# Batches 0 and 1 kept split in DRAM, the second MLP seven steps behind, the last heads' scaling between two steps

## The reference

```python
# layer 0: cross attention (16 heads of 16), then an MLP
q = ln(x) @ Wq;  k, v = split(ln(context) @ Wkv)
x = x + softmax(q k^T * 0.25) v @ Wproj + bproj
x = x + gelu(ln(x) @ W1 + b1) @ W2 + b2
# layer 1: self attention (16 heads of 64), cross attention (16 of 64), gated MLP
x = attn(ln(x), ln(x), Wq1, Wk1, Wv1, Wo1, bo1) + x
x = attn(ln(x), context, Wq2, Wk2, Wv2, Wo2, bo2) + x
a, gate = split(ln(x) @ Wp + bp)
x = x + (a * gelu(gate)) @ Wf + bf
```

## Time and profile before

| | us |
|---|---|
| median of 3 runs | 2421.74 (2419.34 to 2422.18) |
| profiled execution | 2421.08 |
| its span | 2419.2 |
| PE busy | 2161.0 (89%) |
| DVE busy | 1674.4 (69%) |
| ACT busy | 1310.7 (54%) |
| POOL busy | 1292.6 (53%) |

### The profile page before, as it was taken

One profiled execution on the slowest core, in us unless ns is written; L12 is line 12 of the kernel. 1 busy time (PEld: TensorE's weight loads), 2 busy tenths in 40 slices (PEclk: granted clock), 3 DMA queues, 4 the chain that ended last, 5 costly groups with the idle time before them and its releaser, 6 DMA issues. The chain is left out here.

```text
span 2419.2 us, 31242 instructions
## 1 busy us (share of the span) xinstructions
PE 2161.0 (89%) x11628; PEld 1788.5 (74%) x11628; DVE 1674.4 (69%) x2343; ACT 1310.7 (54%) x1938; POOL 1292.6 (53%) x1013
## 2 busy tenths in 40 slices
PE   6867999997699999999999999999999689999998
PEld 4646888886577777777777777777777578899887
DVE  5457677654777777777777878777776776666654
ACT  5335666643466656565666665565665355555431
POOL 2145455545255556565555656656556676666432
PEclk8968999998899999999999999999999899999999
DMA  6610000011000000000000000000011321111000
GB/s 199 211 39 7 20 20 21 10 53 51 13 23 14 26 25 14 32 14 23 23 14 32 14 18 32 14 23 23 14 34 53 115 81 49 51 52 44 27 9 18
DMA packets 87608, 94.27 MB, mean 39 GB/s; under 512 B 29409, under 2 KB 69089, under 8 KB 87457
## 3 DMA queue, kind: packets, MB, share of 16 engines
q1 hardware_dynamic: 87456, 92.27, 11.7%
HBM read 61.30 MB, written 29.62 MB: 38 GB/s over the span
## 5 line engine op out<-in xcount | busy, mean ns | idle before, releaser
L144 PE MATMUL PS<-R 128*128 128x512 f32 (+1 forms) x2944 | 1033.4, 351 | 138.8 <-DVE R L160 52.5
L145 PE MATMUL PS<-R 128*128 128x512 f32 (+1 forms) x2944 | 1002.5, 341 | 0.0
L146 PE MATMUL PS<-R 128*128 128x512 f32 (+1 forms) x2944 | 1002.5, 341 | 0.0
L144 PEld LDWEIGHTS PS<-R 128*128 128x128 f32 x2944 | 570.5, 194 | 257.2 <-DVE R L160 68.6
L157 POOL TENSOR_SCALAR R<-F 128x1024 fp32r<-128x1024 f32 (+1 forms) x487 | 546.6, 1127 | 346.2 <-DVE F L1775 147.3
L154 ACT ACTIVATE R<-PS 64x512 fp32r<-64x512 f32 (+4 forms) x860 | 460.5, 546 | 385.4 <-PE PS L146 155.1
L146 PEld LDWEIGHTS PS<-R 128*128 128x128 f32 x2944 | 570.0, 194 | 61.6
L145 PEld LDWEIGHTS PS<-R 128*128 128x128 f32 x2944 | 571.7, 194 | 55.2
L160 DVE TENSOR_TENSOR R<-F,R 128x1024 fp32r<-128x1024 f32 (+2 forms) x426 | 528.6, 1245 | 79.0 <-POOL R L157 56.3
L1359 ACT ACTIVATE F<-PS 128x1024 f32<-128x1024 f32 x256 | 263.2, 1028 | 331.5 <-PE PS L1225 204.8
L160 DVE TENSOR_TENSOR R<-PS,R 128x512 fp32r<-128x512 f32 (+3 forms) x348 | 181.9, 543 | 232.4 <-ACT R L154 231.7
(11 more groups left out here) (85 smaller groups left out, 1900.1 us busy)
## 6 DMA issues: line engine op xcount, KB each, us to landing
F<-sd SPq DMA_DIRECT2D x128, 128.0 KB, 2.8
gd<-F SPq DMA_DIRECT2D x8, 1024.0 KB, 4.1
vd<-F SPq DMA_DIRECT2D x8, 1024.0 KB, 4.5
xs<-F SPq DMA_DIRECT2D x16, 512.0 KB, 2.6
F<-xs SPq DMA_DIRECT2D x16, 512.0 KB, 3.6
R<-gd SPq DMA_DIRECT2D x8, 1024.0 KB, 5.8
R<-vd SPq DMA_DIRECT2D x8, 1024.0 KB, 5.7
F<-in_x SPq DMA_DIRECT2D x8, 512.0 KB, 5.5
```

The costliest lines, as they stand in the source:

```text
L144: nc.tensor.matmul(o, L[0], Rr[0], start=start, stop=False, skip_group_check=share)
L145: nc.tensor.matmul(o, L[0], Rr[1], start=False, stop=False, skip_group_check=share)
L146: return nc.tensor.matmul(o, L[1], Rr[0], start=False, stop=stop, skip_group_check=share)
```

## The change

1. *Products.* Batches 0 and 1 get DRAM tensors of their own, `gd2` and `vd2`, that hold hi and lo. ACT rounds these two batches' part straight from PSUM to hi, DVE subtracts for lo, and SP writes both. The plain copies cover the other six batches. The groups of vw are taken in the order of batches 2-3, 4-5, 6-7, 0-1 (`vw5_pair`). The new buffers take the place of the stage in which the weights of this part arrived, so ACT first waits for these weights to be split.
2. *Stage 4, start.* Batches 0 and 1 are loaded as pairs, with twice the bytes, and PE waits for the load itself. Their splits (8 halves on ACT and POOL) are gone from `products_at` and from the outer loop.
3. *Lag.* LAG is 7: the loop has one step fewer, and batch b's first MLP block stands in step 4b+7. The norms stay where they are. The down-projection's residual additions and the stores follow the lag; the weights of the MLP are split one step earlier (4, 3, 3, 3, 3 a step).
4. *Last heads.* `early4_pool = {6: 1, 8: 2, 9: 1}`: on POOL alone, step 3 is moved behind the scaling of the last head pair.

The diff, cut to its core:

```diff
@@ -375,11 +377,14 @@
-            with nc.sbuf_tensor("R0", [128, 6528], FR) as r, nc.sbuf_tensor("F0", [128, 12288], FP) as g:
-                ra, fa = Area(r, 6528), Area(g, 12288)
+            with nc.sbuf_tensor("R0", [128, 6528], FR) as r, nc.sbuf_tensor("F0", [128, 6144], FP) as g:
+                ra, fa = Area(r, 6528), Area(g, 6144)
                 kt5, vb5 = [ra.pair(NT) for _ in range(2)], [ra.pair(8, 128) for _ in range(2)]
-                gs5, vs5 = [fa.take(8, 256) for _ in range(2)], [fa.take(8, 256) for _ in range(2)]
-                stage5 = fa.take(8 * 512)
+                gs5, vs5 = [fa.take(6, 256) for _ in range(2)], [fa.take(6, 256) for _ in range(2)]
+                with nc.sbuf_tensor("S0", [128, 4096], FP) as stage5_at:
+                    stage5 = Area(stage5_at, 4096).take(4096)
+                with nc.sbuf_tensor("S1", [128, 4096], FR) as split5:
+                    gr5, vr5 = [[shaped(split5, 2048 * k + 1024 * i, (2, 2, 256)) for i in range(2)] for k in range(2)]
...
@@ -473,10 +480,13 @@ (sp_products)
-                nc.sync.dma_start(gd[:, :, p, :].rearrange("b p w -> p b w"), gs5[p % 2]).then_inc(g5_out[p % 2].sem, 16)
+                nc.sync.dma_start(gd[2:, :, p, :].rearrange("b p w -> p b w"), gs5[p % 2]).then_inc(g5_out[p % 2].sem, 16)
+                sp.wait_ge(g5_lo, 2 * p + 1)
+                nc.sync.dma_start(gd2[:, :, p].rearrange("b p h w -> p b h w"), f32(gr5[p % 2])).then_inc(g5_out[p % 2].sem, 16)
...
@@ -567,13 +582,19 @@ (act_products)
                 if p >= 0:
+                    wait_weights(act, "k2", "q2", "v2", "o2")
                     act.wait_ge(g5_out[p % 2], p // 2 - 1)
                     act.wait_ge(g5_mm, 2 * p)
                     act_copy(g5_view(gs5[p % 2], 0), g5_bank(0)).then_inc(g5_act.sem, 1)
+                    act_copy(g5_view(gr5[p % 2][:, :, 0, :], 0), g5_bank(0, 0, 2)).then_inc(g5_hi.sem, 1)
+                    act.wait_ge(g5_mm, 2 * p + 1)
+                    act_copy(g5_view(gr5[p % 2][:, :, 0, :], 1), g5_bank(1, 0, 2)).then_inc(g5_hi.sem, 1)
...
+                    act.wait_ge(vw5_mm, 4 * p + 3)
+                    act_copy(vr5[p % 2][:, :, 0, :], vw5_bank(3)).then_inc(vw5_hi.sem, 1)
@@ -608,12 +629,17 @@ (dve_products)
-                    dve.wait_ge(g5_mm, 2 * p + 1)
-                    nc.vector.tensor_copy(g5_view(gs5[p % 2], 1), g5_bank(1)).then_inc(g5_dve.sem, 1)
+                    for k in range(2):
+                        dve.wait_ge(g5_hi, 2 * p + k)
+                        if k == 1:
+                            nc.vector.tensor_copy(g5_view(gs5[p % 2], 1), g5_bank(1)).then_inc(g5_dve.sem, 1)
+                        hi, lo = [g5_view(gr5[p % 2][:, :, h, :], k) for h in range(2)]
+                        dve_rest(lo, g5_bank(k, 0, 2), hi).then_inc(g5_lo.sem, 1)
...
@@ -1115,15 +1141,35 @@
         def sp_keys(b):
...
+            if b < 2:
+                nc.sync.dma_start(to, gd2[b]).then_inc(g_in[b].sem, 16)
+            else:
+                nc.sync.dma_start(to[:, :, 1, :], gd[b]).then_inc(g_in[b % 2].sem, 16)
...
+        def wait_keys(queue, b):
+
+            if b < 2:
+                queue.wait_ge(g_in[b], 0)
+            else:
+                queue.wait_ge(g_lo, 2 * b - 3)
...
-        early4 = {6: 1, 8: 3}
+        early4, early4_pool = {6: 1, 8: 3}, {6: 1, 8: 2, 9: 1}
...
@@ -1395,9 +1441,6 @@ (act_attention1)
-                    if tail3(s, j) == 4:
-                        act_keys(0, 0)
-                        act_keys(0, 1)
...
@@ -1530,10 +1573,7 @@ (pool_attention1)
-                    if tail3(s, j) == 4:
-                        pool_keys(0, 0)
-                        pool_keys(0, 1)
-                    for _ in range(early4.get(tail3(s, j), 0)):
+                    for _ in range(early4_pool.get(tail3(s, j), 0)):
                         next(ahead)
...
-        N4, LAG = 4 * NB, 8
+        N4, LAG = 4 * NB, 7
...
         def products_at(i):
 
-            if i == 1:
-                return [("k", 1, 0), ("v", 0, 0), ("v", 0, 1)]
-            if i in (3, 4, 5):
-                return [[], [("v", 1, 0)], [("v", 1, 1), ("k", 2, 0)]][i - 3]
             kind, b = ("k", i // 4 + 1) if i % 4 in (1, 2) else ("v", (i + 1) // 4)
-            return [(kind, b, int(i % 4 in (0, 2)))] if 1 < i and b < NB else []
+            return [(kind, b, int(i % 4 in (0, 2)))] if 2 <= b < NB else []
 
         def weights_at(i):
-            return g5[3 * i - 6:3 * i - 3] if 2 <= i < LAG else []
+            return g5[3 * i - 5 if i > 2 else 0:3 * i - 2] if 2 <= i < LAG else []
...
-                if i % 4 == 0 and i >= LAG + 4:
+                if (i - LAG) % 4 == 0 and i >= LAG + 4:
                     sp_store(3, (i - LAG - 4) // 4, out, res4, 2 * ((i - LAG - 4) // 4) + 1)
...
-                pe.wait_ge(g_lo, 2 * b + 1)
+                wait_keys(pe, b)
```

More of the change, by code:

```diff
@@ L452, in build @@
         g5_mm, g5_act, g5_dve = event("g_mm", 16), event("g_act", 8), event("g_dve", 8)
+        g5_hi, g5_lo, vw5_hi = event("g_hi", 16), event("g_lo", 16), event("vw_hi", 8)
         vw5_mm, vw5_act, vw5_dve = event("vw_mm", 32), event("vw_act", 16), event("vw_dve", 16)
-        g5_out = [event(f"g_out{i}", 4, 16) for i in range(2)]
-        vw5_out = [event(f"vw_out{i}", 4, 16) for i in range(2)]
+        g5_out = [event(f"g_out{i}", 4, 32) for i in range(2)]
+        vw5_out = [event(f"vw_out{i}", 4, 32) for i in range(2)]
         def sp_products():
@@ L523, in pe_products @@
                         pe.wait_ge(yn_hi, 1)
-                        for b in (2 * i, 2 * i + 1):
+                        for b in (2 * vw5_pair(i), 2 * vw5_pair(i) + 1):
                             m = mm3(bank(6 + i % 2)[:, 256 * (b % 2):256 * (b % 2) + 256], [v[:, b, :] for v in vb5[p % 2]],
@@ L530, in g5_view, with g5_bank, vw5_pair @@
             return v.rearrange("p b (k a s) -> p k a b s", k=2, a=2)[:, k]
-        def g5_bank(k):
-            return bank(2 + 2 * k, 2).rearrange("p (a b s) -> p a b s", a=2, b=NB)
+        def g5_bank(k, lo=2, hi=NB):
+            return bank(2 + 2 * k, 2).rearrange("p (a b s) -> p a b s", a=2, b=NB)[:, :, lo:hi, :]
+        def vw5_pair(i):
+            return (i + 1) % 4
         def vw5_bank(i):
@@ L1116, in build, with wait_values @@
         g_in, v_in = [[event(f"{n}_in{i}", NB // 2, 16) for i in range(2)] for n in ("g", "v")]
-        g_hi, g_lo, vw_hi, vw_lo = [event(n, 2 * NB) for n in ("g_hi", "g_lo", "vw_hi", "vw_lo")]
+        g_hi, g_lo, vw_hi, vw_lo = [event(n, 2 * NB - 4) for n in ("g_hi", "g_lo", "vw_hi", "vw_lo")]
         def sp_keys(b):
-            nc.sync.dma_start(f32(g_b[b % 2])[:, :, 1, :, :].rearrange("p a k w -> p a (k w)"), gd[b]).then_inc(g_in[b % 2].sem, 16)
-        def sp_values(b):
-            nc.sync.dma_start(f32(vw_b[b % 2])[:, :, 1, :], vd[b]).then_inc(v_in[b % 2].sem, 16)
+            to = f32(g_b[b % 2]).rearrange("p a h k w -> p a h (k w)")
+            if b < 2:
+                nc.sync.dma_start(to, gd2[b]).then_inc(g_in[b].sem, 16)
+            else:
+                nc.sync.dma_start(to[:, :, 1, :], gd[b]).then_inc(g_in[b % 2].sem, 16)
+        def sp_values(b):
+            if b < 2:
+                nc.sync.dma_start(f32(vw_b[b]), vd2[b]).then_inc(v_in[b].sem, 16)
+            else:
+                nc.sync.dma_start(f32(vw_b[b % 2])[:, :, 1, :], vd[b]).then_inc(v_in[b % 2].sem, 16)
+        def wait_keys(queue, b):
+            if b < 2:
+                queue.wait_ge(g_in[b], 0)
+            else:
+                queue.wait_ge(g_lo, 2 * b - 3)
+        def wait_values(queue, b):
+            if b < 2:
+                queue.wait_ge(v_in[b], 0)
+            else:
+                queue.wait_ge(vw_lo, 2 * b - 3)
         def act_keys(b, half):
@@ L1133, in pool_keys @@
         def pool_keys(b, half):
-            pool.wait_ge(g_hi, 2 * b + half)
+            pool.wait_ge(g_hi, 2 * b - 4 + half)
             v = g_b[b % 2][:, 4 * half:4 * half + 4]
@@ L1143, in pool_values @@
         def pool_values(b, half):
-            pool.wait_ge(vw_hi, 2 * b + half)
+            pool.wait_ge(vw_hi, 2 * b - 4 + half)
             v = vw_b[b % 2][:, 4 * half:4 * half + 4]
```

15 lines of the change are left out of this document (10 added, 5 removed).

## The result

| | before | changed |
|---|---|---|
| median of 20 runs each, us | 2421.35 (2418.61 to 2429.88) | 2430.1 (2423.2 to 2436.28) |
| profiled execution, us | 2421.08 | 2425.76 |
| its span, us | 2419.2 | 2423.9 |

The ratio of the changed kernel to the one before is 1.0033, 95% interval 1.0022 to 1.0044: slower by 8 us, where 6.4 was forecast. The two profiled executions are only 4.7 us apart. Lines of the changed kernel are two or more further down: L162 and L165 are the rests on DVE and POOL, L640 the copy of a group of vw, L1803 and L1884 the softmax lines, L1499 and L1563 a head pair's reciprocal and scaling.

A forecast was written before the change was run, and what follows sets the result against it. TensorE is busy 89% of the span, so only its waits count. The terms 4.2 - 12.6 + 2.7 + 12.1 = +6.4 us on 2421.08 gave 2427.5, forecast as 2428; 8-in-10 range 2416 to 2436.

The forecast's parts named there:

- Part 4: Steady steps and tail: with lag seven PE waits for the MLP norm's split, 1.3 us six times and 4.0 once; +12.1 us.
- rival C: Steady steps and tail: the clock falls at the new waits, 2 us lost at each of seven, 2442 us; chance 10%.
- Part 1: Product stage, 40 to 105 us: extra DVE rests add 0.41 us per head pair, plus ScalarE's last rounding; +4.2 us.
- The 0.9 behind the last pair: End of the product stage: one more 512-element rounding on ScalarE before the next layer's weights; +0.9 us.
- Parts 2 and 3: Entry into stage 4: removed roundings and rests against doubled matrix loads; 9.9 us gained net.
- Part 2: Entry into stage 4: roundings and rests of batches 0 and 1 go, POOL is reordered, PE waits less; -12.6 us.
- Part 3: Entry into stage 4: batch 0's doubled loads delay a head pair's small transfers and the first exponential; +2.7 us.
- another 3.6 us: Entry, between the third output and step 8: further gain from a wait, a ScalarE rounding and step 7's MLP blocks; 3.6 us.
- 1.6 for the clock: Entry into stage 4: 1.6 us of half speed taken off the gain for the slower granted clock.
- A: Steady steps and tail: the norm's split is in time, so the lag costs 0 and the time is 2416 us; chance 15%.
- B: Product stage and entry: the rests lie in DVE's gaps and small transfers are not held up, 2421 us; chance 20%.
- D: Entry: POOL's new order fails, the last head's scaling still comes late and 3.5 us return, 2431 us; chance 5%.

The follow-up runs named there:

- e1: The changed kernel with a lag of eight instead of seven, all else kept: 2417.2 us, ratio 0.9975 to the kernel before.
- e3: The changed kernel, lag still seven, with POOL's norm split put ahead of the second MLP block's rounding: 2418.6 us, ratio 0.9981 to the kernel before.
- e4: The changed kernel with both small product-stage rests on DVE behind the copy PE waits for: 2425.5 us, ratio 1.0007 to the kernel before.
- e9: The changed kernel with a lag of eight and both product-stage rests behind the copy PE waits for: 2411.7 us, ratio 0.9954 to the kernel before.
- e5: The changed kernel with lag eight and batch 0's values loaded behind the last-but-one head pair's sums: 2421.1 us, ratio 0.9977 to the kernel before.
- e7: The changed kernel with lag eight, rests behind the copy, batch 0's values and batch 1's keys loaded later: 2417.8 us, ratio 0.9956 to the kernel before.
- e8: The kernel before with only POOL's new order at the entry into stage 4: ratio 0.9996 to the kernel before.
- e6: The changed kernel with lag eight and POOL's old order at the entry: 2423.5 us, ratio 0.9991 to the kernel before.
- e10: The changed kernel with lag eight, the same code measured once more: ratio 0.9971 to the kernel before.

## Why the prediction was right

Direction and size were right: +6.4 us forecast, +8 by the ratio, +4.7 between the profiled executions. By its own steps:

- **Part 4, the lag, +12.1: right, and the cause of the sign.** Six times 1.33 us, by the order of one engine's jobs read off, and a wait of 3.86 in the tail for 4.0 forecast. e1 gives 12 to 14 us back and e3 shows the mechanism. The form was right too: the gap shows as 1.05 us idle, for 1.3 forecast; what the 0.28 more is by which each batch falls back was not settled. With the 1.4 us of slower clock behind the tail's wait, which the forecast had left to rival C, the part cost 13.4.
- **Part 1, the product stage, +4.2: the 0.41 per pair was exact.** The 0.9 behind the last pair came as 0.8: PE's wait for DVE there is 3.19 us for 2.38. How much of it reaches the end is not shown. Between the profiled executions the shift is 3.6 to 4.3 us from 124 to 174 us and 1.5 from 219 on, while the granted clock from 110 to 170 us differs (0.67 before, 0.73 changed). e1 has the same product stage; it leaves it 3.0 us late and is only 0.2 late at 131 us. Against that, the ratios of e4 and e9 gain 4 to 6 us for 0.63 per pair, with intervals of some 4 to 5 on either side, which speaks for most of it arriving. Single profiled executions can't settle that.
- **Parts 2 and 3, the entry: 9.9 net, right in sum.** The same working as in the account above gives 10.2 in the changed kernel, 9.6 in e4, whose entry has the same code, and 9.9 in e3, which differs in step 6 alone. Inside the sum two errors cancelled, and that was luck.
- **Part 2, -12.6: its last step failed.** Up to the third output product the forecast had 10.6 us less part 3's 2.7, so 7.9; measured are 11.2 in the changed kernel and 9.0 to 9.6 in e4 and e3, so this stretch gave more than forecast. The failing step is the one behind it, "another 3.6 us" up to step 8 less 1.6 for the clock, +2.0: from there to step 10 the lead, with the two blocks counted, changed by -1.0 in the changed kernel, +0.6 in e4 and +0.3 in e3. The third and later outputs there wait 1.5 to 2.4 us for DVE, as they did before, and the clock stayed at 0.80 for a further 25 us instead of recovering. In e1, where the order of the MLP is as before, the lead is 9.2 us at the third output product, 7.5 two steps on and 8.7 at the end; the windows there differ in clock too.
- **Part 3, the backlog, +2.7: the mechanism right, the size open.** The reciprocal, counted from the fourth last head pair's, came 1.9 us later in the changed kernel (34.6 for 32.7) and 3.9 in e1, for 3 to 4.5 forecast. The first exponential came only 0.9 later (44.2 for 43.4) in the changed kernel, 2.9 in e1. No run here takes the backlog away without putting it elsewhere (e5, e7), so no run shows what the term is worth at the end.
- **What the entry's gain comes from**, which the forecast gave in one sum: by the rest of the span the order of POOL alone brings 5.1 (e8), the matrices kept split alone 0.7 (e6, within the spread), both together 7.7 to 8.7 (e1, e10). So the matrices bring 2.6 to 3.6 once POOL has its new order. The edit with the most code behind it has the smaller gain there, and pays 3.3 us in the product stage.
- **Rivals.** A, the norm in time: no, seven waits after step 8. B, hidden extras: the rests are not hidden in the stage (e4); whether the backlog is hidden at the end is open. C, the clock falling at the new waits: no at the six short ones, yes at the tail's, the place that C named as the likeliest, with 0.83 and 1.4 us here and 0.71 and 2.8 in e4; C had put 2 us on each wait. D, the order of POOL without effect: no (e6).

## What to carry to other kernels

When work is moved one step closer to what feeds it, write down for the feeding engine the order of its jobs in that step: here a split stood behind two roundings that nobody waited for, and putting it first was worth as much as undoing the move. Place new small operations behind the instruction that the busiest engine waits for, not in program order of their data. And when a big load is moved out of the way of one small transfer, look at which transfers it now stands ahead of: the sums came 3 us earlier, the weights of the MLP 3 us later, and the time did not change.

## What the runs showed of the hardware

The same code (e1 and e10) ran 9.4 us apart up to the fourth last head pair. Part of it arises in layer 0. The same two exponentials in e1 and in e10:

```profile
280.16 1.06 ACT L933 ACTIVATE F<-F 128x1024 f32<-128x1024 f32 x1 [1.89 <-DVE F L995]
...
385.59 1.06 ACT L933 ACTIVATE F<-F 128x1024 f32<-128x1024 f32 x1 [1.90 <-DVE F L995]
```

```profile
284.98 1.06 ACT L933 ACTIVATE F<-F 128x1024 f32<-128x1024 f32 x1 [1.90 <-DVE F L995]
...
394.59 1.06 ACT L933 ACTIVATE F<-F 128x1024 f32<-128x1024 f32 x1 [1.89 <-DVE F L995]
```

105.4 us and 109.6. Over 280 to 390 us the granted clock was 0.98 and 0.94:

```profile
280.00:390.00 110.00, 100.15 (x643) 87.11 (x643) 77.58 (x133) 72.44 (x101) 57.60 (x41) 0.98 0.07 23
```

```profile
280.00:390.00 110.00, 100.29 (x615) 87.03 (x614) 75.34 (x130) 68.48 (x97) 55.76 (x41) 0.94 0.07 22
```

PE is busy for 100 us in both and gets, by its records, 28 matmuls fewer done. Which of the two an execution gets decides more of its time than any edit here but the lag, so a single pair of profiled executions can't price an edit by its spans. What puts it into one or the other was not tried.

The loads of 2.1 MB ran at 401 GB/s where those of 1.05 MB had 344. The Trainium skill, "DMA: Bandwidth & Descriptors", section "Measured (HBM→SBUF, 128 partitions, SWDGE, issued from GpSimd)", has larger transfers faster, and the trace agrees in direction; no run here separates the transfer's size from the length of its contiguous pieces.
